# Mamba block between two expert layers on one core: where the weights are loaded, and the order of the merge in the routing stage

## The reference

```python
x = x + 0.5 * ffn(layernorm(x), gate_w, experts)
x = x + mamba(layernorm(x), W_in, conv_w, conv_b, A_log, D, W_out)
x = x + 0.5 * ffn(layernorm(x), gate_w, experts)
```

```python
gate_logits = x @ gate_w                              # 2048 tokens, 8 experts
gates = sinkhorn(gate_logits)                         # 8 rounds of normalisation over tokens and experts
vals, idx = top_k(swapaxes(gates, -1, -2), 256)       # each expert takes its 256 best tokens
routed = x[idx]; outputs = routed @ experts[e] * vals
result = zeros_like(x).at[idx].set(outputs)
```

## Time and profile before

| | |
|---|---|
| median of 3 runs | 3817.17 us (3815.45 to 3819.61) |
| profiled execution, its own time | 3821.82 us |
| its span, first to last instruction | 3820.3 us |
| granted TensorE clock, mean | 0.856 of full speed |
| VectorE busy | 3107.9 us, 81% |
| TensorE busy | 2787.8 us, 73% |
| ScalarE busy | 2135.3 us, 56% |
| GpSimd busy | 1281.8 us, 34% |

### The profile page before, as it was taken

One profiled execution on the slowest core, in us unless ns is written; L12 is line 12 of the kernel. 1 busy time (PEld: TensorE's weight loads), 2 busy tenths in 40 slices (PEclk: granted clock), 3 DMA queues, 4 the chain that ended last, 5 costly groups with the idle time before them and its releaser, 6 DMA issues. The chain is left out here.

```text
span 3820.3 us, 29742 instructions
## 1 busy us (share of the span) xinstructions
PE 2787.8 (73%) x9244; PEld 1524.3 (40%) x9244; DVE 3107.9 (81%) x2624; ACT 2135.3 (56%) x2286; POOL 1281.8 (34%) x900
## 2 busy tenths in 40 slices
PE   8701488899799889889989979997896695025553
PEld 4501233345345445434534634543442454014442
DVE  5798059999999999999999999989999467972222
ACT  6300366876876787688687687678766262001111
POOL 0000247245344443624624434440110100015665
PEclk9655799999999999999989999999998896557776
DMA  6200448778778868867877787886775471024666
GB/s 260 111 0 11 127 113 178 156 162 165 177 171 170 179 147 177 186 145 165 183 161 172 157 177 168 173 175 121 144 139 121 80 286 67 0 92 136 216 217 240
DMA packets 146762, 575.75 MB, mean 151 GB/s; under 512 B 22160, under 2 KB 73936, under 8 KB 99792
## 3 DMA queue, kind: packets, MB, share of 16 engines
q0 software_dynamic: 77568, 402.71, 50.9%
q1 hardware_dynamic: 69072, 171.59, 12.2%
HBM read 154.72 MB, written 117.51 MB: 71 GB/s over the span
## 5 line engine op out<-in xcount | busy, mean ns | idle before, releaser
L1057 DVE TENSOR_TENSOR_SCAN state<-state,drive 128x2048 f32<-128x2048 f32 x512 | 2220.8, 4405 | 75.7 <-ACT state L1222 75.7
L1222 ACT ACTIVATE state<-delta,neg_a 128x2048 f32<-128x2048 f32 x512 | 1020.2, 2003 | 276.1 <-DMA state<-state 186.2
L1393 PE MATMUL ps_states<-state,ident 128*128 128x512 f32 x1800 | 898.5, 646 | 167.6 <-DMA state<-state 167.6
L953 POOL DMA_DIRECT2D state<-state x256 | 232.8, 911 | 1288.9 <-DVE state L1057 1264.3
L1393 PEld LDWEIGHTS ps_states<-state,ident 128*128 128x128 f32 x1800 | 363.9, 209 | 608.4 <-issue 399.1
L1329 PE MATMUL ps_proj<-x1t,w_in 128*128 128x512 f32 x1024 | 502.5, 627 | 77.9 <-ACT conv_in L1138 59.2
L1345 PE MATMUL ps_proj<-conv_in,tap 128*128 128x512 f32 x1024 | 456.9, 594 | 0.5 <-ACT conv_in L1138 0.5
L901 POOL DMA_INDIRECT picked<-normed_rows,slot_now x128 | 368.7, 2880 | 256.0 <-DVE gate_now L995 188.8
L917 POOL DMA_INDIRECT x<-routed_rows,row_now x128 | 334.7, 2615 | 154.5 <-issue 64.3
L1329 PEld LDWEIGHTS ps_proj<-x1t,w_in 128*128 128x128 f32 x1024 | 196.1, 197 | 345.5 <-issue 235.8
L1345 PEld LDWEIGHTS ps_proj<-conv_in,tap 128*128 128x128 f32 x1024 | 191.7, 189 | 245.4 <-issue 244.7
(11 more groups left out here) (267 smaller groups left out, 3177.1 us busy)
## 6 DMA issues: line engine op xcount, KB each, us to landing
state<-state POOLq DMA_DIRECT2D x256, 1024.0 KB, 7.7
delta<-xc POOLq DMA_DIRECT2D x24, 1024.0 KB, 12.3
normed_rows<-rows_in SPq DMA_DIRECT2D x8, 2048.0 KB, 7.5
expert<-in_experts SPq DMA_DIRECT2D x64, 256.0 KB
routed_rows<-routed SPq DMA_DIRECT2D x128, 128.0 KB
x<-in_x POOLq DMA_DIRECT2D x16, 1024.0 KB, 10.6
x_rows<-x SPq DMA_DIRECT2D x16, 1024.0 KB, 7.8
x_rows<-rows_out POOLq DMA_DIRECT2D x64, 256.0 KB, 8.6
```

The lines of the kernel that those rows point to most:

```text
L953: nc.gpsimd.dma_start(out=state[held(q)][:], in_=state[held(q - 1)][:], accum_op=ALU.add).then_inc(pair_landed(b, q // 2)[0], 16)
L1057: nc.vector.tensor_tensor_scan(state[held(q)][:], state[held(q)][:], drive[j % 2][:], 0.0, ALU.mult, ALU.add).then_inc(state_ready, 1)
L1222: nc.scalar.activation(state[held(q)][:], delta[j % 2][:], ACT.Exp, scale=g.neg_a[:, j, n:n + 1]).then_inc(decay_ready, 1)
L1393: mm = nc.tensor.matmul(ps_sum[c][:], g.ident[:], state[held(q)][:, c * CH:(c + 1) * CH], start=(opening and n == 1), stop=(n == N - 1))
```

## The change

The five weights of the mixer are issued by SyncE in the gates stage of the first `route`, behind the loads of the first four batches of x, and awaited at the end of SyncE's part of that stage. `constants` awaits the zeros only. The gate weights get a semaphore of their own, and TensorE and VectorE wait for it ahead of their first use.

The merge keeps its values and the number of its instructions. The shift of the indices is formed as gap * above + min(gap, 0) * equal in two tiles (`swap` or `spare`, and `other`) that are added; instructions are issued in another order, "above" of a level ahead of the last two of the level in front; and each waits only for the ones that it reads from (`after`).

```diff
@@ constants, sync
-            sp.dma_start(g.gate_w[:], ...).then_inc(loaded, 16)
-            sp.dma_start(g.w_in[:], w.w_in_t.rearrange("(k p) c -> p k c", p=P)).then_inc(loaded, 16)
-            sp.dma_start(g.w_out[:], ...).then_inc(loaded, 16)
-            sp.dma_start(g.conv_w[:], ...).then_inc(loaded, 16)
-            sp.dma_start(g.conv_b[:], w.conv_b_t).then_inc(loaded, 16)
-            sp.dma_start(g.skip[:], w.skip_t).then_inc(loaded, 16)
+            sp.dma_start(g.gate_w[:], ...).then_inc(g.gate_loaded, 16)
             sp.wait_ge(zeroed, 1)
             for table in g.routed:
                 sp.dma_start(table[0:E, :], zrow[:]).then_inc(zero_stored, 16)
-            sp.wait_ge(loaded, 6 * 16)
             sp.wait_ge(zero_stored, NB * 16)
@@ gates_stage, sync
         for b in range(1, U):
             sp.dma_start(rows_[b][:], x_in[b]).then_inc(row_in[b], 16)
+        if tag == "in":
+            w = g.weights
+            sp.dma_start(g.w_in[:], ...).then_inc(g.loaded, 16)
+            sp.dma_start(g.w_out[:], ...).then_inc(g.loaded, 16)
+            sp.dma_start(g.conv_w[:], ...).then_inc(g.loaded, 16)
+            sp.dma_start(g.conv_b[:], w.conv_b_t).then_inc(g.loaded, 16)
+            sp.dma_start(g.skip[:], w.skip_t).then_inc(g.loaded, 16)
         for b in range(NB):
...
         for u in range(U):
             sp.wait_ge(row_out[u], 16 * NB // U)
+        sp.wait_ge(g.loaded, 5 * 16)
@@ gates_stage, vector
         dve.wait_ge(summed, 1)
+        dve.wait_ge(g.gate_loaded, 16)
@@ gates_stage, tensor
+        pe.wait_ge(g.gate_loaded, 16)
         for k in range(KD):
@@ top_stage, vector (merge and exchange go)
+        def after(*made):
+            dve.wait_ge(merge_step, max(made))
+
+        def index_shift(ab, eq, gp, one, two, filler):
+            after(ab, gp)
+            a = step_of(nc.vector.tensor_tensor(one, buf_gap, buf_above, ALU.mult))
+            after(eq, gp)
+            b = step_of(nc.vector.scalar_tensor_tensor(two, buf_gap, 0.0, buf_equal, ALU.min, ALU.mult))
+            more = filler()
+            after(a, b)
+            return step_of(nc.vector.tensor_tensor(one, one, two, ALU.add)), more
...
+        ab = step_of(nc.vector.tensor_tensor(buf_above, yv, xv, ALU.is_gt))
+        eq = step_of(nc.vector.tensor_tensor(buf_equal, yv, xv, ALU.is_equal))
+        after(moved_i)
+        gp = step_of(nc.vector.tensor_tensor(buf_gap, yi, xi, ALU.subtract))
+        high = step_of(nc.vector.tensor_tensor(merged_v[0][:], xv, yv, ALU.max))
+        shift, _ = index_shift(ab, eq, gp, swap[:], other[:], lambda: 0)
+        after(shift)
+        high_i = step_of(nc.vector.tensor_tensor(merged_i[0][:], xi, swap[:], ALU.add))
...
+        after(high)
+        ab = step_of(... "above" of the first level ...)
+        for n in range(1, M.bit_length()):
+            d = M >> n
...
+            after(high, low)
+            eq = step_of(nc.vector.tensor_tensor(buf_equal, pairs(v, 1), pairs(v, 0), ALU.is_equal))
+            after(high_i, low_i)
+            gp = step_of(nc.vector.tensor_tensor(buf_gap, pairs(i, 1), pairs(i, 0), ALU.subtract))
+            high = step_of(nc.vector.tensor_tensor(pairs(v2, 0), pairs(v, 0), pairs(v, 1), ALU.max))
+            shift, low = index_shift(ab, eq, gp, one, two, lambda: step_of(
+                nc.vector.tensor_tensor(pairs(v2, 1), pairs(v, 0), pairs(v, 1), ALU.min)))
+            if d > 1:
+                after(high, low)
+                d = d // 2
+                ab = step_of(nc.vector.tensor_tensor(pairs(above, 0), pairs(v2, 1), pairs(v2, 0), ALU.is_gt))
+                d = M >> n
+            after(shift)
+            high_i = step_of(nc.vector.tensor_tensor(pairs(i2, 0), pairs(i, 0), one, ALU.add))
+            low_i = step_of(nc.vector.tensor_tensor(pairs(i2, 1), pairs(i, 1), one, ALU.subtract))
+        after(high, low, high_i, low_i)
```

More of the change, by code:

```diff
@@ L85, in constants @@
         ctx.enter_context(nc.semaphore(n)) for n in ("passed_dve", "passed_pool", "passed_sp"))
+    g.loaded, g.gate_loaded = (ctx.enter_context(nc.semaphore(n)) for n in ("weights_loaded", "gate_loaded"))
     with ExitStack() as c2:
@@ L89, in constants @@
         zeroed = c2.enter_context(nc.semaphore("zeroed"))
-        loaded = ctx.enter_context(nc.semaphore("weights_loaded"))
         a_loaded = c2.enter_context(nc.semaphore("a_log_loaded"))
@@ L115, in _ @@
             sp.dma_start(g.neg_a[:], w.A_log.rearrange("(j p) n -> p j n", p=P)).then_inc(a_loaded, 16)
-            sp.dma_start(g.gate_w[:], w.gate_w.rearrange("(k p) e -> p k e", p=P)).then_inc(loaded, 16)
-            sp.dma_start(g.w_in[:], w.w_in_t.rearrange("(k p) c -> p k c", p=P)).then_inc(loaded, 16)
-            sp.dma_start(g.w_out[:], w.w_out_t.rearrange("(j p) d -> p j d", p=P)).then_inc(loaded, 16)
-            sp.dma_start(g.conv_w[:], w.conv_w.rearrange("(j p) k -> p j k", p=P)).then_inc(loaded, 16)
-            sp.dma_start(g.conv_b[:], w.conv_b_t).then_inc(loaded, 16)
-            sp.dma_start(g.skip[:], w.skip_t).then_inc(loaded, 16)
+            sp.dma_start(g.gate_w[:], w.gate_w.rearrange("(k p) e -> p k e", p=P)).then_inc(g.gate_loaded, 16)
             sp.wait_ge(zeroed, 1)
@@ L229, in _ @@
             sp.dma_start(rows_[b][:], x_in[b]).then_inc(row_in[b], 16)
+        if tag == "in":
+            w = g.weights
+            sp.dma_start(g.w_in[:], w.w_in_t.rearrange("(k p) c -> p k c", p=P)).then_inc(g.loaded, 16)
+            sp.dma_start(g.w_out[:], w.w_out_t.rearrange("(j p) d -> p j d", p=P)).then_inc(g.loaded, 16)
+            sp.dma_start(g.conv_w[:], w.conv_w.rearrange("(j p) k -> p j k", p=P)).then_inc(g.loaded, 16)
+            sp.dma_start(g.conv_b[:], w.conv_b_t).then_inc(g.loaded, 16)
+            sp.dma_start(g.skip[:], w.skip_t).then_inc(g.loaded, 16)
         for b in range(NB):
@@ L471, in top_stage @@
     merged_i = [sb(f"merged_i{i}", [R, M]) for i in range(2)]
-    above, equal, swap, gap = (sb(n, [R, M]) for n in ("above", "equal", "swap", "gap"))
+    above, equal, swap, gap, other, spare = (sb(n, [R, M]) for n in ("above", "equal", "swap", "gap", "other", "spare"))
     half_turned, half_copied, mirrored, merge_step = (
@@ L528, in _, with step_of @@
         n_merge = [0]
[L530 to L552, removed]
+        def step_of(ins):
+            ins.then_inc(merge_step, 1)
+            n_merge[0] += 1
+            return n_merge[0]
@@ L556, in _ @@
         dve.wait_ge(mirrored, 1)
-        merge(nc.vector.tensor_scalar(merged_i[1][:], ps_mirror[0:R, M:2 * M], float(T // 2), None, ALU.add))
+        moved_i = step_of(nc.vector.tensor_scalar(merged_i[1][:], ps_mirror[0:R, M:2 * M], float(T // 2), None, ALU.add))
         dve.wait_ge(idx_conv, 1)
[L559 to L569, removed]
@@ L570, in _ @@
-        assert now == FINAL
+        xv, xi, yv, yi = vals[0:R, :], idx_f[0:R, :], ps_mirror[0:R, 0:M], merged_i[1][:]
+        buf_above, buf_equal, buf_gap = above[:], equal[:], gap[:]
+        ab = step_of(nc.vector.tensor_tensor(buf_above, yv, xv, ALU.is_gt))
[3 more added lines that the diff above has]
+        high = step_of(nc.vector.tensor_tensor(merged_v[0][:], xv, yv, ALU.max))
@@ new lines, in _, with pairs @@
+        shift, _ = index_shift(ab, eq, gp, swap[:], other[:], lambda: 0)
+        after(shift)
+        high_i = step_of(nc.vector.tensor_tensor(merged_i[0][:], xi, swap[:], ALU.add))
+        low, low_i = high, high_i
+        def pairs(buf, k):
+            return buf[:].rearrange("r (a k d) -> r a k d", k=2, d=d)[:, :, k, :]
+        d = M // 2
+        after(high)
+        ab = step_of(nc.vector.tensor_tensor(pairs(above, 0), pairs(merged_v[0], 1), pairs(merged_v[0], 0), ALU.is_gt))
+        for n in range(1, M.bit_length()):
+            d = M >> n
+            v, i, v2, i2 = merged_v[(n - 1) % 2], merged_i[(n - 1) % 2], merged_v[n % 2], merged_i[n % 2]
+            one, two = pairs(swap, 0) if n % 2 else pairs(spare, 0), pairs(other, 0)
+            buf_above, buf_equal, buf_gap = (pairs(buf, 0) for buf in (above, equal, gap))
+            after(high, low)
[13 more added lines that the diff above has]
+            low_i = step_of(nc.vector.tensor_tensor(pairs(i2, 1), pairs(i, 1), one, ALU.subtract))
@@ L1632, in program @@
     with ExitStack() as ctx:
+        g.weights = w
         constants(nc, g, w, ctx)
```

## The result

Measured side by side, the changed kernel takes 3802.81 us (median of 8) and the kernel before 3818.39 (median of 8). The ratio is 0.9956, 95% interval 0.9945 to 0.9967, or 16.8 us less (12.6 to 21.0); by the medians it is 15.6. The prediction was 3805.2 us, 11.9 less than a median of 3817.2.

The account below looks back on a forecast made before the run. VectorE's mixer scans dominate but are untouched; the touched start and routing stretches are serial. 3.3 + 8.6 = 11.9 us off the profiled 3821.8 gives 3809.9, the median 4.65 lower: 3805.2 us, range 3799 to 3812.

Parts of the forecast that it names:

- What bounds: First 11 us and a 25 us stretch in each routing stage: serial, so each microsecond removed comes off the time.
- Part 1: Merge in both routing stages: reordered so that other instructions cover the waits; gain 4.3 us per stage, 8.6 us in all.
- the step: Levels of the merge: 78 steps at 0.209 us and one at 0.315, so 16.6 us instead of 20.48.
- The exchange: Ahead of the merge's levels, on 256 columns: 3.28 us instead of 3.69, gain 0.4 us.
- Part 2: Start of the kernel: weights moved, zeros issued 3.2 us earlier, gates stage begins at 7.8 us; gain taken 3.3 us.
- Up to 0.7: Landing of the zeros at the start: up to 0.7 us shorter than 2.6 us.
- The five loads behind x: First gates stage, SyncE: 3.2 us of weight issue hidden in its idle time; no loss taken, upper bound 4 us.
- Nearly nine times: SyncE's idle 27.3 us before the first normalised batch: 3.2 us of weight issue fit in nearly nine times.
- A: Rival on the merge: covered waits no cheaper than direct ones, or order gives nothing; 3813.9 us, chance 0.10.
- B: Rival at the start: gates stage doesn't begin earlier, or x mixed with weights gives 3.3 us back; 3808.6, chance 0.06.
- C: Rival in the last stage: slower through TensorE's clock, at 0.60 21 us more and 3826; chance 0.03.
- The signs: Expected in the trace: gates stage at 7.5 to 8 us, first merge level about 2.1, store wait above 20, mixer unchanged.

Follow-up runs that it names:

- merge only: The kernel before with the new merge alone, weights loaded and awaited where they were: 3746.27 us against 3758.58, ratio 0.9968.

## Why the prediction was right, point by point

- What bounds: right. The stretches that the change touches are serial, and nothing says that their gain is lost behind them: 14.5 us in the trace, 12.6 to 21 in the runs.
- Part 1, that a covered wait is free: right, and shown by the same order with direct waits. The size was 4.3 us a stage, measured 4.85. The term that was mis-sized is the step: I took 0.209 us from the spacing behind an instruction that waited directly, and all steps are 0.202 (315.48 to 331.03 us in 77 of them). 78 x 0.007 is the 0.5 us. The exchange was right: 3.24 us (312.24 to 315.48), 3.28 predicted.
- Part 2: right in sign, 4.8 us instead of 3.3. The issue moved by 3.2 us as worked out; the landing fell from 2.6 to 1.0 us, not by a share of the 0.7 us that I gave it. It is 1.0 us in the later traces of this start too, and 2.9 in merge only, where the weights stand in front. The zeros had stood behind the weights in the DMA engines, whose share was 0.97 between 6 and 7 us in the kernel before and is 0.10 between 4 and 5 us in the changed one. "Up to 0.7" counted only what the engines still moved after SyncE's last issue.
- The five loads behind x: hidden, as predicted, but their issue was mis-sized by a factor of six (20 us, not 3.2), since I took it from an empty queue. "Nearly nine times" was 1.4 times: 28.1 us from the first of them to the first store, 20.2 of them in use. One more issue like conv_b's would have made the store late, so that they stayed hidden owes something to luck.
- TensorE's clock. I gave it a rival in the last stage only. It acts in the first gates stage, where the trace of after is 2.4 us longer, with a low stretch of 6.8 us from 63.8 us on. The identical kernel lost nothing against the one before in its second trace (174.1 us against 174.7), and low stretches are no effect of the change: before has one of 3.4 us at 97.4 us, merge only one at 69.3. But one of 6.8 us stands in two of the five traces with late weights and idle waits and in neither of the two without, so whether the new start makes the long one likelier stays open.
- Rivals: A is refuted by the steps of 0.20 us and by the direct waits, B by the start of the gates stage at 6.3 us in every trace of this start. C did not come: the last stage took 402 us after 406, at a clock of 0.72 after 0.71.
- The signs. As told: the last zeros issued by 4.8 us, about 2.1 us per ten instructions (2.03), scans unchanged (2482.3 us after 2483.1), no longer wait for the second batch of x. Not as told: the gates stage begins at 6.2 us and not at 7.5 to 8, conversion to last index instruction is 19.3 us and not 19.9, and SyncE's wait ahead of the first store is 7.8 us (30.0 to 37.84) and not above 20.
- The sum of 11.9 us against 14.5 in the trace: the steps make 1.1 of the difference, the landing 1.5. Both errors made the forecast too small, so they didn't cancel. The runs would allow a few microseconds more than 14.5, and what these would be isn't shown.

## What to carry to other kernels

Where small operations on one engine depend on each other, put an independent one between producer and consumer and wait for the producer's own count, not for everything issued: here that is 0.11 us a step at 128 elements, with no instruction less. A queue that serves loads and stores should issue a load as soon as its buffer is free, ahead of waits for work that it doesn't need; this was worth 10 to 12 us, against some 14.5 of the whole change. Work out a moved DMA's issue time from a queue as full as the one it moves to.

## What was not expected of the hardware

- A DMA issue of 2 KB on SyncE took 12.7 us behind 8 MB of loads of x, and 0.8 in an emptier queue.
- TensorE behind a wait of some 3 us ran at 1.2 GHz for 0, 3.4 or 6.8 us in executions whose gates stage has the same code.
- The last stage takes 402 and 406 us in the first two traces and 343 to 346 in the ten of the later jobs, with the same instructions and all other stages equal to a few us. That it is the chip is inferred; it was not tried.
